# Self queries and keys laid on their quads' rows by DMA instead of by 16 matrix products, and self attention begun behind fewer waits

## The reference

```
x = x + selfattention(layernorm(x))           # causal; q, v, k = h @ Wqvk
x = x + crossattention(layernorm(x), context) # q = h @ Wq + bq; k, v from the context with biases
x = x + experts(layernorm(x))                 # router, top 2 of 8 experts of width 512
```

## Time and profile before

| | us |
|---|---|
| median of 3 runs | 946.25 (946.11 to 951.87) |
| profiled execution, whole | 945.66 |
| its span | 942.5 |
| PE busy in the span | 868.7 (92%) |
| ACT busy in the span | 841.0 (89%) |
| first exponential of self attention | 67.33 after the span's start |

### The profile page before, as it was taken

The page is one execution under the profiler, slowest core; times in us unless marked ns, Lnnn a source line. Parts: engine busy times, 40 slices in busy tenths (PEclk is TensorE's granted clock), DMA queues, the critical chain, the costliest instruction groups (busy, mean ns, idle before and its releaser), DMA issues.

```text
span 942.5 us, 15734 instructions
## 1 busy us (share of the span) xinstructions
PE 868.7 (92%) x6269; PEld 274.7 (29%) x6269; DVE 373.2 (40%) x789; ACT 841.0 (89%) x702; POOL 46.7 (5%) x104
## 2 busy tenths in 40 slices
PE   6977888998899999999999999999999999998997
PEld 4562222222222222222222232232222322222543
DVE  5765644331499469929972120110010001000432
ACT  5667987999999999999999999999999999998432
POOL 4000000000000000000000013000000000010300
PEclk9998999999999999999999999999999999999999
DMA  4253004711121111122112214223333210110120
GB/s 150 97 201 59 1 1 129 233 35 34 37 38 34 34 37 39 41 56 41 37 34 38 37 40 138 37 59 57 57 60 59 59 55 34 56 63 15 36 100 13
DMA packets 24812, 56.14 MB, mean 60 GB/s; under 512 B 6986, under 2 KB 12084, under 8 KB 24476
## 3 DMA queue, kind: packets, MB, share of 16 engines
q1 hardware_dynamic: 21276, 44.18, 19.0%
q0 software_dynamic: 3456, 10.88, 4.0%
HBM read 37.59 MB, written 9.59 MB: 50 GB/s over the span
## 4 chain that ended last, share of the span: by engine, by line
PE 45%; ACT 27%; DVE 14%; issue 12%; DMA 1%; SPq 0%; ACTq 0%; DVEq 0%
ACT probs L862 27%; PE psum L1685 18%; PE psum L1649 10%; PE psum L1980 3%; PE psum L1988 3%; DVE kparts_bc L1153 2%; DVE w_quads L1153 2%; DVE attnT L1142 2%; DVE attnT L1143 2%; PE psum L1923 2%; PE psum L1518 1%; PE psum L1558 1%; PE psum L1562 1%; PE psum L1805 1%; DVE attnT L1147 1%
## 5 line engine op out<-in xcount | busy, mean ns | idle before, releaser
L862 ACT ACTIVATE probs<-psum 128x1536 f32<-128x1536 f32 x570 | 773.6, 1512 | 28.4 <-PE psum L1649 14.2
L1685 PE MATMUL psum<-probs,v_ctx 128*9 128x512 f32 x3128 | 409.3, 595 | 2.7 <-DVE turned L1100 2.4
L1649 PE MATMUL psum<-q_all,k_ring 32*128 32x512 f32 (+1 forms) x1756 | 290.3, 487 | 44.3 <-ACT probs L862 40.6
L1649 PEld LDWEIGHTS psum<-q_all,k_ring 32*128 32x128 f32 x1756 | 111.9, 183 | 429.2 <-ACT probs L862 389.0
L1685 PEld LDWEIGHTS psum<-probs,v_ctx 128*9 128x9 f32 x3128 | 46.5, 88 | 102.2 <-issue 96.5
L1100 DVE STREAM_TRANSPOSE turned<-psum 128x512 f32<-128x512 f32 x16 | 11.5, 717 | 135.2 <-PE psum L1681 120.1
L933 ACT ACTIVATE probs<-psum,b_sb 128x512 f32<-128x512 f32 x32 | 22.0, 687 | 33.8 <-PE psum L1980 33.8
L1153 DVE SCALAR_TENSOR_TENSOR kparts_bc<-kparts_bc,attnT 128x512 f32<-128x512 f32 x60 | 41.5, 692 | 2.0
L1685 PE MATMUL psum<-probs,v_self 128*9 128x512 f32 (+3 forms) x384 | 40.3, 519 | 1.8 <-DVE probs L1121 1.2
L1416 DVE COPY kparts_bc<-psum 128x128 f32<-128x128 f32 x11 | 3.2, 292 | 96.5 <-PE psum L1923 96.5
L739 POOL DMA_INDIRECT block_rows<-xn,slots x8 | 7.9, 984 | 549.0 <-DVE slots L1387 546.8
(11 more groups left out here) (227 smaller groups left out, 555.7 us busy)
## 6 DMA issues: line engine op xcount, KB each, us to landing
k_ring<-kc_parts SPq DMA_DIRECT2D x256, 52.0 KB
k_ring<-kc_parts SPq DMA_DIRECT2D x256, 48.0 KB
kc_parts<-kparts_bc SPq DMA_DIRECT2D x8, 512.0 KB, 2.8
q_all<-w_region POOLq DMA_DIRECT2D x13, 256.0 KB, 3.6
q_all<-ctx_region POOLq DMA_DIRECT2D x13, 256.0 KB, 4.1
kc_parts<-probs SPq DMA_DIRECT2D x4, 512.0 KB, 3.5
w_region<-in_L_ffn_W SPq DMA_DIRECT2D x1, 2048.0 KB, 9.9
probs<-gate_rows SPq DMA_DIRECT2D x2, 1024.0 KB, 5.7
```

The costliest lines, as they stand in the source:

```text
L862: act.activation(probs[:, slot:slot + w, :], psum[:, at:at + w, :], ACT.Exp, scale=SC[ph]).then_inc(L[ph]["exp_done"], 1)
L1649: mm = pe.matmul(into[:, col:col + n_q], keys, q_all[rows, g, hf * HALF + q0:hf * HALF + q0 + n_q], start=True, stop=True)
L1685: mm = pe.matmul(into[:, q0:q0 + w], v_all[:, h, t, :], probs[:, place(ph, at)[1], col:col + w], start=first, stop=last)
```

## The change

- `self_quads` goes: 16 products (32 instructions), their 16 ACT copies and 16 DVE splits, and the eight ACT copies that made `w_quads` for them. Instead the four plain products that were already there for the squares (`QK_BANKS`, bank 3 becomes 2) are each rounded by ACT (`evac` in `self_squares`) and split by DVE (`qkself_split`), 4 + 4 instructions, into `self_parts`.
- SP stores these parts to a new DRAM array `qk_dram` in eight DMAs of 256 KB, after the store of chunk 0 (`store_self_parts`), waits until all of them have landed, and loads them onto the rows of `q_all` and `k_self` in 64 DMAs (`load_self_quads`), each eight partitions x four quads x 512 tokens, 64 KB. Six of them follow the store of each chunk (`SELF_LOADS`), the last four that of chunk 10. They share SP's queue with the chunk stores, which come between them.
- The buffers of `kparts` change places, so that the one in `probs` belongs to chunks 1, 4, 7 and 10; the key banks of odd and even chunks are swapped.
- PE begins self attention when `qk_loaded` counts all 64 loads and chunk 11 is split, scores group 0, and only then does the last norm products, waits for the last chunk (`context_read`) and scores group 1. ACT waits for the norms and the stores of `kparts[1]` only at group 2 of the exponentials; the waits for the other stores go to DVE's `query_squares`. The verdict is loaded by ACT and DVE inside the chunk loop. DVE reduces bank 7 of the norms, clears the output bank, and reduces bank 6 afterwards. ACT makes the cross weights (`quad_weights(2, ...)`) at chunk 8 and not behind the loop.

```diff
+SELF_LOADS = 6
-QK_BANKS = (3, 5, 0, 1)
+QK_BANKS = (2, 5, 0, 1)
+def kctx_bank(c):
+    return 3 - c % 2
...
-        kparts = [kparts_a, kparts_bc[:, 0], kparts_bc[:, 1]]
+        kparts = [kparts_bc[:, 0], kparts_a, kparts_bc[:, 1]]
+        self_low = probs[:, 11:15, :].rearrange("p (w a) c -> p w (a c)", w=2)
+        self_parts = ((attnT[:, :], self_low[:, 0, :]),
+                      (heads[:, :, :, :].rearrange("p c g d -> p (c g d)"), self_low[:, 1, :]))
...
+            def store_self_parts(hf):
+                sp.wait_ge(s["qkself_split"], 2 * hf + 2)
+                here = slice(hf * HALF, (hf + 1) * HALF)
+                for which in range(2):
+                    for part in range(PARTS):
+                        sp.dma_start(qk_dram[which, part, :, here], self_parts[which][part][:, here])\
+                            .then_inc(s["qk_stored"], 16)
+            def load_self_quads(n):
+                hf, which, r, j = n // 32, n // 16 % 2, n // 4 % 4, n % 4
+                if n == 0:
+                    sp.wait_ge(s["qk_stored"], 16 * 2 * 2 * PARTS)
+                row, here = ROWS * r + HD * j, slice(hf * HALF, (hf + 1) * HALF)
+                part = j // 2 if which else j % 2
+                sp.dma_start((q_all, k_self)[which][row:row + HD, :, here].bitcast(F32),
+                             qk_dram[which, part, :, here].rearrange("(g r d) c -> r d g c", g=QUADS, r=LANES)[r])\
+                    .then_inc(s["qk_loaded"], 16)
+            loaded = 0
             for c in range(NCHUNK):
                 w = min(CHUNK * P, KV - c * CHUNK * P)
                 sp.wait_ge(s["kctx_split"], c + 1)
                 sp.dma_start(...).then_inc(s[f"kctx_stored{c % KRING}"], 16)
+                if c == 0:
+                    for hf in range(NHALF):
+                        store_self_parts(hf)
+                for n in range(loaded, min(loaded + SELF_LOADS, 2 * 32)):
+                    load_self_quads(n)
+                loaded += SELF_LOADS
...
             act.wait_ge(s["wself_loaded"], 16)
-            quad_weights(0, wqvk_sb[:, 0:D], Q_SIGNS, s["wself_quads"])
-            quad_weights(1, wqvk_sb[:, 2 * D:3 * D], K_SIGNS, s["wself_quads"])
...
+                evac(self_parts[n % 2][0][:, here].bitcast(F32R), bank(QK_BANKS[n]), s["qkself_high"])
...
-            for m in range(4 * QUADS):
-                act.wait_ge(s["qkquad_ps"], m + 1)
-                if m >= 2:
-                    act.wait_ge(s["qkquad_split"], m - 1)
-                evac(high[:, m % 2, :].bitcast(F32R), bank(QK_BANKS[m % 4]), s["qkquad_high"])
...
+                if c == 6:
+                    self_bounded = verdict_of(act, 0)
+                if c == 8:
+                    act.wait_ge(s["wlate_loaded"], 16 * LATE)
+                    quad_weights(2, wq_sb[:, :], [sign * QUERY_SCALE for sign in Q_SIGNS], s["wcross_quads"])
...
+            def squares_read():
+                act.wait_ge(s["norms_ctx"], 1)
+                act.wait_ge(s["kctx_stored1"], 16 * len(range(1, NCHUNK, KRING)))
...
+                    if ph == 0 and g == 2:
+                        squares_read()
...
-            for n in range(KRING):
-                act.wait_ge(s[f"kctx_stored{n}"], 16 * len(range(n, NCHUNK, KRING)))
-            choose(act, 0, lambda: exponentials(0, 0, n_groups(0)), lambda: general_exponentials(0))
+            act.cond(self_bounded, lambda: exponentials(0, 0, n_groups(0)), general_self)
...
-            for m in range(4 * QUADS):
-                g, which, hf = m // 4, m // 2 % 2, m % 2
-                dve.wait_ge(s["qkquad_high"], m + 1)
-                dst = (q_all, k_self)[which][:, g, hf * HALF:(hf + 1) * HALF]
-                step(dve.scalar_tensor_tensor(dst, bank(QK_BANKS[m % 4]), low[:, which:which + 1], high[:, m % 2, :],
-                                              ALU.mult, ALU.subtract), "qkquad_split")
+            for n in range(4):
+                dve.wait_ge(s["qkself_high"], n + 1)
+                here = slice(n // 2 * HALF, (n // 2 + 1) * HALF)
+                step(dve.tensor_tensor(self_parts[n % 2][1][:, here].bitcast(F32R), bank(QK_BANKS[n]),
+                                       self_parts[n % 2][0][:, here], ALU.subtract), "qkself_split")
...
             dve.wait_ge(s["norms_ctx"], 1)
+            norm_columns(bank(7), (KT + 1) * H - HALF, 2)
+            dve.memset(bank(OUT_BANK), 0.0).then_inc(s["outs_cleared"], 1)
             norm_columns(bank(6), HALF, 0)
-            norm_columns(bank(7), (KT + 1) * H - HALF, 2)
-            dve.memset(bank(OUT_BANK), 0.0).then_inc(s["outs_cleared"], 1)
...
-            pe.wait_ge(s["wself_quads"], 2 * COPIES)
-            self_quads()
-            pe.wait_ge(s["qkquad_split"], 4 * QUADS)
+            pe.wait_ge(s["qkself_split"], 3)
             transpose_ctx(2)
...
-            pe.wait_ge(s["kctx_split"], NCHUNK)
-            pe.wait_ge(s["vctx_done"], NCHUNK)
-            pe.wait_ge(s["tail_done"], 1)
+            def context_read():
+                pe.wait_ge(s["kctx_split"], NCHUNK)
+                pe.wait_ge(s["vctx_done"], NCHUNK)
+                pe.wait_ge(s["tail_done"], 1)
+            pe.wait_ge(s["qk_loaded"], 16 * 64)
...
             def self_attention():
-                for group in range(2):
-                    score_group(0, group)
+                pe.wait_ge(s["kctx_split"], NCHUNK - 1)
+                score_group(0, 0)
+                last_norms()
+                context_read()
+                score_group(0, 1)
                 attention(0, first_half, 0, n_groups(0))
```

More of the change, by code:

```diff
@@ L340, in decoder_layer @@
         turned = sb("turned", [P, NHALF, HALF])
-        high = turned
         wqvk_sb = sb("wqvk_sb", [D, 3 * D])
@@ L452, in decoder_layer @@
         qs_dram = nc.dram_tensor("qs_parts", (H * ROWS, SEQ), F32).ap()
+        qk_dram = nc.dram_tensor("self_parts", (2, PARTS, D, SEQ), F32).ap()
         kc_dram = nc.dram_tensor("kc_parts", (PARTS, D, KV), F32).ap()
@@ L463, in decoder_layer @@
             "x_loaded0 x_loaded1 wself_loaded ctx_loaded0 ctx_loaded1 ctx_loaded2 ctx_loaded3 wctx_loaded ctail_loaded wlate_loaded wffn_loaded "
-            "ident_made rows_made consts_made outs_cleared ones_made dve_step wself_quads wcross_quads "
-            "norm_done normT_ps normT_done qkself_ps qkquad_ps qkquad_high qkquad_split vself_ps vself_done "
+            "ident_made rows_made consts_made outs_cleared ones_made dve_step wcross_quads "
+            "norm_done normT_ps normT_done qkself_ps qkself_high qkself_split qk_stored qk_loaded vself_ps vself_done "
             "ctxT_ps ctxT_done ctailT_done kctx_ps kctx_first kctx_split vctx_ps vctx_done tail_done ktail_loaded "
@@ L614, in load_general_self @@
             def load_general_self():
-                sp.wait_ge(s["qkquad_split"], 4 * QUADS)
+                sp.wait_ge(s["qk_loaded"], 16 * 64)
                 store_parts(0, ks_dram, k_self)
@@ L814, in ctx_keys @@
                 act.wait_ge(s["kctx_ps"], c + 1)
-                act.activation(sq_ctx[:, c * CHUNK * P:c * CHUNK * P + w], bank(2 + c % 2)[:, 0:w], ACT.Square)\
+                act.activation(sq_ctx[:, c * CHUNK * P:c * CHUNK * P + w], bank(kctx_bank(c))[:, 0:w], ACT.Square)\
                     .then_inc(s["sq_ctx"], 1)
@@ L818, in ctx_keys @@
                     act.wait_ge(s[f"kctx_stored{c % KRING}"], 16 * (c // KRING))
-                evac(kparts[c % KRING][:, 0, 0:w].bitcast(F32R), bank(2 + c % 2)[:, 0:w], s["kctx_first"])
+                evac(kparts[c % KRING][:, 0, 0:w].bitcast(F32R), bank(kctx_bank(c))[:, 0:w], s["kctx_first"])
             for c in range(2):
@@ L894, in general_exponentials, with general_self @@
                             ins.then_inc(G[ph]["turned"], 1)
-            for n in range(KRING):
-                act.wait_ge(s[f"kctx_stored{n}"], 16 * len(range(n, NCHUNK, KRING)))
-            choose(act, 0, lambda: exponentials(0, 0, n_groups(0)), lambda: general_exponentials(0))
+            def general_self():
+                squares_read()
+                general_exponentials(0)
+            act.cond(self_bounded, lambda: exponentials(0, 0, n_groups(0)), general_self)
             exponentials(1, 0, PART_AT)
@@ L992, in ctx_keys_split @@
                 dve.wait_ge(s["kctx_first"], c + 1)
-                step(dve.tensor_tensor(kparts[c % KRING][:, 1, 0:w].bitcast(F32R), bank(2 + c % 2)[:, 0:w],
+                step(dve.tensor_tensor(kparts[c % KRING][:, 1, 0:w].bitcast(F32R), bank(kctx_bank(c))[:, 0:w],
                                        kparts[c % KRING][:, 0, 0:w], ALU.subtract), "kctx_split")
@@ L1042, in _ @@
                 ctx_values(c)
+                if c == 7:
+                    self_bounded = verdict_of(dve, 0)
             dve.wait_ge(s["consts_made"], N_CONSTS)
@@ L1051, in _ @@
             dve.wait_ge(s["norms_ctx"], 1)
-            norm_columns(bank(6), HALF, 0)
             norm_columns(bank(7), (KT + 1) * H - HALF, 2)
```

(13 more changed lines are left out.)

4 lines of the change are left out of this document (removed).

## The result

| | before | after |
|---|---|---|
| median | 947.37 us (946.11 to 951.87, 4 runs) | 960.2 us (956.67 to 961.15, 4 runs) |
| ratio | | 1.0126, 95% interval 1.009 to 1.0163 |
| profiled execution, its span | 945.66, 942.5 us | 961.15, 959.4 us |
| first exponential of self attention | 67.33 us | 79.12 us |

Forecast were 960.7, from the median of 946.25 over three runs, and the first exponential at 81.7. The executions of after lie 1.75 us over their span (961.15 against 959.4) and not 3.2 as before, so 1.4 of the 16.9 us of span are not in the time. On a second chip the same kernel came out a little nearer (e5_after_again: 957.2 against 948.04, ratio 1.0076, 1.0046 to 1.0105).

A forecast was written before the change was run, and what follows sets the result against it. Before self attention, quads on PE and the last store's landing bound; afterwards the 64th load's landing. 35.7 + 31.5 loads + 13.1 stores + 0.5 = 80.8, first exponential 81.7, +14.4 us: 960.7 us, range 948.5 to 975.

The forecast's parts named there:

- Start of the loads: On SP's queue, behind the first chunk store and eight part stores: first load at about 34.8 us, data moving from 35.7.
- Rate of the loads: 64 loads of 4.19 MB, held by eight engines, at the 133 GB/s of 48 earlier piece loads: 31.5 us.
- the 38.5 us: Estimate for the 64 loads from the port limit, two at a time on different ports; would make the time 968.
- The chunk's own chain hides: In the context loop: rounding chunk c waits only for the store three chunks back, so it adds no time.
- First exponential: Start of self attention, after the last load and scoring: at 81.7 us instead of 67.33, +14.4 us.
- Self attention zero, -2 to +1.5: Self attention behind its start: no net change; first value product 1 to 1.5 us late, up to 2 us given back.
- the clock would be given back: Start of self attention: PE restarts before the exponentials, so the earlier low-clock stretch may give back up to 2 us.
- The stretch behind the first exponential unchanged within 2 us: Profile sign: from first exponential of self attention to the kernel's end, the time stays the same within 2 us.
- the full rate: Rival: the self loads run at 200 GB/s, 21.0 us, +3.9 us, time 950.1; chance 0.18.
- all engines share the loads: Rival: loads spread over all 16 engines, SP's issue sets the pace, exponential at 64.8, -2.5 us, 943.7; chance 0.07.
- The slow rate: Rival: the self loads run at 94 GB/s throughout, 44.6 us, +27.5 us, time 973.8; chance 0.25.
- SP did not need longer for a load with four blocks: Rival: SP's issue takes 0.66 us a load, ending at 81.1, as late as the forecast; no chance of its own given.

The follow-up runs named there:

- e5_after_again: The changed kernel itself, run again on a second chip against the kernel before: 957.2 us against 948.04, ratio 1.0076.
- e3: Changed kernel with PE's last norm products and the waits for the last chunk ahead of the wait for the loads: 953.64 us, ratio 1.0072 to the kernel before.
- e7: Changed kernel with the 31 late weight loads issued by POOL instead of SP: 955.03 us, ratio 1.0065 to the kernel before.
- e6: Changed kernel with last norms ahead of the wait for the loads, plus eight unused products on PE: 964.02 us, ratio 1.0152 to the kernel before.
- e8: Kernel before with only the new self-attention start, plus an unused PE product and groups 2 to 4 scored twice: 944.08 us, ratio 0.9953.
- e10: Kernel before with only the new start of self attention, repeated on a third chip: 941.87 us against 946.59, ratio 0.9955.
- e1: Changed kernel with the same 64 loads, each moving 256 of its 512 tokens: 946.87 us against 945.7 for the kernel before, ratio 0.9997.
- e9: Changed kernel with 32 loads on 16 partitions, four a chunk, and late weight loads issued by POOL: 949.73 us against 946.59 for the kernel before, ratio 1.002.
- e2: Changed kernel with 32 loads of 128 KB on 16 partitions, three a chunk, keys' parts stored twice: 950.29 us, ratio 1.0038 to the kernel before.
- e4: Kernel before, quads made by products, with only the new start of self attention: 942.57 us against 945.7, ratio 0.9952.

## Why the prediction was right, and where not

The time and the side were right, and the mechanism was: the 64 loads, held by half of the engines, land long after the quads would have been done. Its signs came: the first load at 34.63, chunk 12 split before the last load landed, PE's wait ended by that load, the clock at 0.50 when scoring began. Point by point:

- *Start of the loads:* 34.8 forecast, 34.63 measured; the queue ahead (26.38), the engines' time for eight stores and the landing were each as reckoned. SP issued the part stores at 0.47 to 0.71 and not 0.41, which the transfers hid.
- *Rate of the loads:* 31.5 us at 133 GB/s forecast, 28.8 us at 146 by the estimate above; measured is the sum with the stores, 41.9 and not 44.6 us. This is the mis-sized term: the last load landed at 78.1 and not at 80.8. The row it was taken from, 48 piece loads, was the nearest; its own rise from 110 to 150 came again (111 GB/s in 36 to 38, later 271 with the stores in it). (The Trainium skill, "SBUF — State Buffer", section "Door 1: The DMA port swizzle": the 38.5 us worked out from it, an estimate, is not borne out by the 28.8.)
- *The chunk's own chain hides:* it did not quite. "Three chunks back" was reckoned with a store's latency of 2.8 us; it became 8.8 to 10.9, and SP waited for splits. It is in the chain above. Forecast were 4.2 us for six loads and a store throughout. They took 2.6 to 3.0 while the buffers were free (36.69 to 45.16), then 4.6 (45.16 to 49.73), and 3.35 later (60.79 to 64.13).
- *First exponential:* +14.4 forecast, +11.8 measured.
- *Self attention zero, -2 to +1.5:* +1.6, just past the end of its range, and -0.1 in e5, the same kernel: single executions differ by that much here. The argument that the clock would be given back was wrong: PE was at work again at 78.28, and the clock stayed low until 90. e3 and e5 speak against DVE's order as a source.
- *The stretch behind the first exponential unchanged within 2 us:* not in this profile, where it is 5.2 longer. Beside the 1.6, 3.6 us are lost at about the 350th exponential, in a place that the change doesn't touch:

```profile
585.23 0.80 PE L1686 MATMUL psum<-q_all,k_ring 32*128 32x512 f32 x3 [1.36 <-issue]
```

PE idles for 1.36 us that no wait in the profile explains. By stretch, first after and then before at about the same work, 14 us earlier:

```profile
584.00:586.00 2.00, 0.77 (x7) 0.33 (x11) 0.00 (x0) 2.00 (x2) 0.96 (x1) 0.71 0.19 66
586.00:588.00 2.00, 2.00 (x14) 0.30 (x11) 0.00 (x0) 1.84 (x2) 1.25 (x1) 0.50 0.03 8
```

```profile
570.00:572.00 2.00, 2.00 (x22) 0.49 (x14) 0.00 (x0) 2.00 (x3) 1.47 (x2) 1.00 0.10 33
572.00:574.00 2.00, 1.73 (x14) 0.31 (x11) 0.00 (x0) 2.00 (x2) 0.66 (x1) 1.00 0.29 88
```

The clock falls to 0.50 behind the gap and PE is behind ACT for some microseconds. The same loss is in e5 (3.7 us) and e7 (4.7), half of it in e6 and e8 (1.8), none in the other six profiled kernels and none in the profile of before. POOL issues eight indirect DMAs just ahead of it, but it does so in before and in e10 too, without a gap. As the four of the second chip all have the loss, e8 without the new loads too, and none on the two others, it is not shown to be the change's; the kernel before was not profiled on that chip. The cause is open.

So 960.2 against 960.7 is partly luck. In the profiled pair 2.6 us too much at the start, and 1.4 that lie outside of the span, stand against 1.6 in self attention and 3.6 behind it. In medians the change cost 12.8 us in the first comparison and 9.2 on the second chip, where 14.4 were forecast: too dear by 1.6 to 5.2 us. The forecast was good to about 5 us, not to 0.5.

The rivals: the full rate (950.1) was wrong for the whole, though the loads came near it late. That all engines share the loads did not happen; whether 64 loads on all engines would have reached its 943.7 was not run. e1, with half of the bytes, speaks against it: SP's pace was 2.95 us a chunk and not 2.6, and the exponential came at 71.5, not 64.8. The slow rate (973.8) did not hold for longer than the first microseconds. SP did not need longer for a load with four blocks: 0.364 us on average, as reckoned.

## What to carry to other kernels

Before work of a busy engine is replaced by DMAs, add up when the last DMA can land: the queue ahead, the landing of what it reads, bytes over the engines that its partitions get, and the other transfers among them. 13.9 us of matrix products gave way to loads that, with the stores between them, took 42 us. Test the parts of a change apart: here one was worth -0.5% and was hidden in a +1.3%. And compare the k-th instruction of a long loop in both traces: it shows at once where a difference arises, and that a sum which comes out right may hold errors that cancel.

## What I had not expected of the hardware

- With transfers queued behind each other a 512 KB store's landing went from 2.8 us to as much as 10.9 us in after and up to 12.3 in e9, at an unchanged size.
- Sixteen engines shown as busy (share 1.01 to 1.09 in e2 and e9) moved anything from 181 to 360 GB/s; the share says who is occupied, not what is moved.
- Issuing a DMA on SP in after cost 0.364 us on average for an 8 x 4 x 512 load (most about 0.31, one 1.10), 0.41 for a chunk store, and 0.47 to 0.71 for the 256 KB part stores.
- The granted clock was at 0.50 in stretches in which PE was busy throughout (e8, 70 to 72 us), after it had fallen where PE was busy for 1.14 of 2 us; and it stayed at 1.00 where PE was busy for only 0.63 of 2 us (e4, 80 to 82).
